# Gate and number operations of a mixture-of-experts kernel in groups of four tiles, and the adds of output pairs one operation a step

## The chip, the core and the metric

The kernel runs on one NeuronCore of a Trainium2 chip, as one program. The metric is the device time in microseconds. Before the change three runs took 502.27, 503.56 and 506.07 us; their median is 503.56 us.

The engines run their own instruction streams and wait for one another through semaphores: TensorE (PE: matrix products), VectorE (DVE), ScalarE (ACT), GpSimd (POOL) and SyncE (SP), which here only issues DMAs.

## The reference, cut to what matters

```
x = x + gnn(layernorm(x), adj)          # 4096 nodes, 256 features, adjacency 4096 x 4096
# ffn(layernorm(x)): 8 experts, the best two for each node
logits = xf @ Wg + bg
topk_scores, topk_idx = top_k(logits, 2)
topk_w = softmax(topk_scores)
h = gelu(einsum('nd,edh->neh', xf, W1) + b1)
y = einsum('neh,ehf->nef', h, W2) + b2
sel = take_along_axis(y, topk_idx[:, :, None], axis=1)
out = sum(topk_w[:, :, None] * sel, axis=1)
x = x + out
```

The kernel computes an expert only for the rows that chose it.

## The kernel before, in words

The first 350 us make the graph layer, choose the experts and write each node's row twice to a DRAM buffer, `dispatched`, sorted by expert: the row (as two f16 parts), its destination number (TOK), its first choice (EXP0), the weight of the first choice (W0) and the difference of the two weights (DW).

The expert stage then runs over ET = 39 tiles of 256 sorted rows, in steps numbered t, software-pipelined by hand; the order on each engine is that of the code, one step after the other:

- SP, `load_rows(t)`: loads tile t's rows to slot t % 8 of `erow` (shown as `stage` in the trace; erow, ehid, ehl and exT all lie in it). From t = 8 on it waits until tile t - 8 is transposed (s_etp) and its gates and numbers are made (s_idc).
- TensorE, step t: transposes tile t (L1329), hidden product of tile t - 1 (L1342, 12 matmuls), output product of tile t - 2 (L1362, 12 matmuls).
- VectorE, step t: COPY of the transposed tile t (L1114); output rows of tile t - 3 with scale and bias into `ysb` (L1122, shown as `rows`); low f16 part of the hidden values of tile t - 1 (L1129, waits for ScalarE's L776); then the gate operations of tile j = t - 1: L1137 and L1142 make `gate`, the weight of each row, and L1139 makes `enum`, the row of `pair_out` that the result goes to. `combine(k)`, in steps 32, 33, 35, 36 and 38 for groups 0 to 4 and behind step 41 for groups 5 and 6, adds the two expert results of 512 nodes (group k) to `x_sb`, with one operation for each (L1153, L1155).
- ScalarE, step t: GELU of tile t (L771, two operations), high f16 part (L776), then `gate_rows(t - 2)`: the output rows times their gates (L760, two operations; waits for L1122 and s_idc).
- GpSimd, `scatter(t)`: two indirect DMAs (L651) that write the 256 weighted rows of tile t to `pair_out` in DRAM. It waits for ScalarE's L760 and s_idc.

Behind the tiles, `pair_out` is read back in NG = 8 groups of 512 nodes (`load_pairs(k)` on SP, L510; the last in two halves, L513) to a ring of four buffers (in `z_lo` and `maskT`), when all tiles that can hold rows of it are scattered and, from k = 4 on, when group k - 4 is added (s_o2). SP's order is: loads 0 to 3 between the last row loads; load 4, write 0; load 5, writes 1, 2; load 6, writes 3, 4, 5; load 7; write 6; write of the last group's halves. `write_out(k)` (L519) waits for the second add of group k. The final group is added in halves (L1169, L1171).

Of the kernel before, what the change touches and what calls it, by code (L numbers as in the profile page):

```python
# [6 lines left out]
ALU = mybir.AluOpType  # L7
# [9 lines left out]
P = 128  # L17
# [6 lines left out]
def gnn_moe_kernel(nc, x, adj, W_self, b_self, W_nb, b_nb, W_comb, b_comb, Wg, bg, W1, b1, W2, b2, out):  # L24
# [47 lines left out]
    with ExitStack() as ctx:  # L72
# [112 lines left out]
        RY = 8  # L185
        tab = sb("tab", [P, 2, ET], I32)
        padrow = sb("padrow", [P, E], I32)
        enum = sb("enum", [P, RY, 2], I32)
        gate2 = sb("gate2", [P, 2, 2], F32)
        gate = sb("gate", [P, RY, 2], F32)  # L190
# [253 lines left out]
        def _(sp):  # L444
# [34 lines left out]
            def load_rows(t):  # L479
                if t == 0:  # L480
                    sp.wait_ge(s_sc[0], 16 * NT)
                if t == EA:
                    sp.wait_ge(s_dum, 16 * DUM)
                    sp.wait_ge(s_padw, 16 * E)
                    sp.wait_ge(s_tab, 4)
                    sp.wait_ge(s_sc[1], 16 * NT)
                if t == R:
                    sp.wait_ge(s_padr, 1)
                    for e in range(E):
                        write_pad(sp, e)  # L490
                a = t % R
                if t >= R:
                    sp.wait_ge(s_etp, t - R + 1)
                    sp.wait_ge(s_idc, t - R + 1)
                    apart(sp)
                row = sp.value_load(tab[0:1, 0, at(t)], min_val=0, max_val=ROWS - TT)
                sp.dma_start(erow_f[:, a], xs_dram[bass.ds(row, TT), :].rearrange("(p s) n -> p s n", s=2)).then_inc(s_er[a], 16)
                if t == R - 1:
                    sp.wait_ge(s_mm, NT)
                    sp.dma_start(b2_bc[:, :, :].rearrange("p e n -> p (e n)"),  # L500
                                 b2.rearrange("(o e) n -> o (e n)", o=1).to_broadcast((P, E * H))).then_inc(s_b2, 16)
# [33 lines left out]
        def _(pool):  # L535
# [110 lines left out]
            def scatter(t):  # L646
                a = t % RY
                pool.wait_ge(s_idc, t + 1)
                pool.wait_ge(s_gt, t + 1)
                for s in range(2):  # L650
                    gp.indirect_dma_start(  # L651
                        out=yp_dram[:, :], out_offset=bass.IndirectOffsetOnAxis(ap=enum[:, a, s:s + 1], axis=0),
# [7 lines left out]
        def _(act):  # L660
# [93 lines left out]
            def gate_rows(j):  # L754
                a = j % RY
                act.wait_ge(s_ey, j + 1)
                act.wait_ge(s_idc, j + 1)
                apart(act)
                for s in range(2):
                    last = sc.activation(ysb[:, a, s, :], ysb[:, a, s, :], ACT.Copy, scale=gate[:, a, s:s + 1])  # L760
# [32 lines left out]
        def _(dve):  # L793
# [313 lines left out]
            def expert_step(t, u, known):  # L1107
# [17 lines left out]
                if live(known, 1, ET):  # L1125
# [7 lines left out]
                    a, b = j % RY, j % R  # L1133
                    if j >= RY:
                        dve.wait_ge(s_ysc[a], 32 * (j // RY))
                    apart(dve)
                    v.scalar_tensor_tensor(gate2[:, r, :], erow32[:, b, :, EXP0], texp[:, at(j)], erow_f[:, b, :, DW],  # L1137
                                           ALU.not_equal, ALU.mult).then_inc(s_g2, 1)
                    v.scalar_tensor_tensor(enum[:, a, :], erow32[:, b, :, EXP0], texp[:, at(j)], erow32[:, b, :, TOK],  # L1139
                                           ALU.not_equal, ALU.add)  # L1140
                    dve.wait_ge(s_g2, j + 1)
                    v.tensor_tensor(gate[:, a, :], gate2[:, r, :], erow_f[:, b, :, W0], ALU.add).then_inc(s_idc, 1)  # L1142
                if known == 1:
                    table_late()
                if known in COMBINE:
                    combine(COMBINE.index(known))

            COMBINE = (32, 33, 35, 36, 38, 41)

            def combine(k):  # L1150
                dve.wait_ge(s_yl[k % Y], 16 * (k // Y + 1))
                xk = x_sb[:, B * k:B * k + B, :]
                v.tensor_tensor(xk, xk, yin[k % Y][:, :, 0, :], ALU.add).then_inc(s_o1, 1)  # L1153
                dve.wait_ge(s_o1, k + 1)
                v.tensor_tensor(xk, xk, yin[k % Y][:, :, 1, :], ALU.add).then_inc(s_o2, 1)  # L1155
# [7 lines left out]
            for k in range(len(COMBINE), NG - 1):  # L1163
                combine(k)
# [231 lines left out]
```

## Time and profile before

| | |
|---|---|
| median of three runs | 503.56 us |
| profiled execution, in all | 508.38 us |
| its span, first to last instruction | 505.0 us |
| TensorE busy | 436.5 us, 86% |
| VectorE busy | 371.1 us, 73% |
| GpSimd busy | 334.5 us, 66% |
| ScalarE busy | 259.7 us, 51% |
| mean granted TensorE clock | 0.946 |

A timeline row gives the start in us from the span's start, the duration, the engine, the line of the kernel, the operation, output and input names, and, in brackets, how long the engine had been idle before it and what ended this. A line L1129 is line 1129 of the kernel before. The engines overlap consecutive instructions, so the start of one to the start of the next tells what it occupies, not its duration. The 39 steps of the expert stage lie between 350 and 485 us of the span.

### The profile page before, as it was taken

What the parts mean: (1) busy time and instruction counts of PE and PEld (TensorE: products, weight loads), DVE (VectorE), ACT (ScalarE), POOL (GpSimd) and SP (SyncE); (2) the same over time, 40 slices, a digit from 0 to 9 for tenths busy, and PEclk for the clock granted to TensorE, in tenths of its full rate; (3) what the DMA queues carried; (4) which work ended last, traced back from release to release, by engine and by line L of the source; (5) the groups of instructions that cost most, each with busy time, mean ns of one, the idle gap of its engine ahead of it and who ended that gap; (6) DMA issues with size and microseconds to landing.
All of it is one profiled execution on the core that took longest, in us unless ns stands there. A gap on an engine that the chain in (4) does not pass through costs nothing.

```text
span 505.0 us, 12812 instructions
## 1 busy us (share of the span) xinstructions
PE 436.5 (86%) x4214; PEld 384.7 (76%) x4214; DVE 371.1 (73%) x1056; ACT 259.7 (51%) x403; POOL 334.5 (66%) x348
## 2 busy tenths in 40 slices
PE   5789999889999889999979969964899999997710
PEld 5678988778888778988858858863799999996610
DVE  2898754577878977798569489766777777779972
ACT  2666872245543524344434443233588888886620
POOL 3498586165666877778658756366788788885570
PEclk9999999999999979999989979985799999999985
DMA  8997899889996999899999997196865556598665
GB/s 222 278 302 230 214 234 286 223 247 264 275 278 181 311 265 257 245 276 291 298 279 275 291 301 216 43 297 209 286 199 174 174 173 186 174 324 346 195 218 166
DMA packets 48687, 122.47 MB, mean 243 GB/s; under 512 B 10601, under 2 KB 19693, under 8 KB 47600
## 3 DMA queue, kind: packets, MB, share of 16 engines
q1 hardware_dynamic: 26736, 64.09, 44.6%
q0 software_dynamic: 16144, 50.49, 33.8%
q10 hardware_dynamic: 5744, 7.08, 5.1%
q8 instruction: 35, 0.57, 0.5%
q14 instruction: 28, 0.23, 0.2%
HBM read 96.52 MB, written 26.93 MB: 244 GB/s over the span
## 4 chain that ended last, share of the span: by engine, by line
DVE 34%; PE 16%; ACT 15%; DMA 13%; issue 10%; POOL 8%; ACTq 2%; DVEq 1%; POOLq 1%; SPq 0%
DMA wst<-in_L_ffn_W_dram 11%; PE bank L1245 7%; ACT stage L771 7%; DVE maskT L845 5%; DVE stage L1129 5%; ACT stage L776 4%; POOL rs L633 3%; DVE x_sb L930 2%; DVE xh L928 2%; DVE w L982 2%; DVE st L934 2%; PE bank L1236 2%; ACT xh L725 2%; PE bank L1237 2%; PE bank L1362 2%
## 5 line engine op out<-in xcount | busy, mean ns | idle before, releaser
L1236 PE MATMUL bank<-z_flat,maskT 128*128 128x257 f16 x1024 | 232.9, 278 | 8.5 <-issue 8.5
L1237 PE MATMUL bank<-z_lo,maskT 128*128 128x256 f16 x1024 | 232.7, 277 | 0.0
L1236 PEld LDWEIGHTS bank<-z_flat,maskT 128*128 128x128 fp8e4 x1024 | 101.9, 100 | 22.9 <-issue 9.0
L651 POOL DMA_INDIRECT pair_out<-rows,enum x78 | 93.6, 1199 | 33.3 <-issue 21.3
L1237 PEld LDWEIGHTS bank<-z_lo,maskT 128*128 128x128 fp8e4 x1024 | 101.8, 99 | 13.2
L676 ACT ACTIVATE mask<-stage,m 128x2048 fp8e4<-128x2048 int32 x32 | 64.1, 2002 | 58.7 <-DMA stage<-in_adj_dram,gidx 47.5
L584 POOL DMA_INDIRECT dispatched<-rows,slot x64 | 65.0, 1016 | 29.4 <-issue 18.2
L573 POOL DMA_INDIRECT stage<-in_adj_dram,gidx x64 | 65.7, 1027 | 26.1 <-issue 13.6
L633 POOL TENSOR_TENSOR rs<-ve,mhalf 128x1 f32<-128x1 f32 x32 | 39.0, 1220 | 49.9 <-DVE ve L939 49.8
L725 ACT ACTIVATE xh<-x_sb,nb,rs 128x256 f32<-128x256 f32 x32 | 19.2, 599 | 100.7 <-POOL nb L635 80.0
L1342 PE MATMUL bank<-stage,w 128*128 128x256 f16 x468 | 59.8, 279 | 4.8 <-DVE stage L1114 4.8
L1362 PE MATMUL bank<-w,stage 128*128 x468 | 57.6, 273 | 3.0 <-DVE stage L1129 2.8
L771 ACT ACTIVATE stage<-bank,b1c,sc 128x256 f32<-128x256 f32 x78 | 43.2, 562 | 21.0 <-PE bank L1342 9.7
L1342 PEld LDWEIGHTS bank<-stage,w 128*128 x468 | 45.2, 100 | 11.1 <-issue 5.5
L1362 PEld LDWEIGHTS bank<-w,stage 128*128 128x128 f16 x468 | 45.3, 98 | 9.4 <-issue 3.8
L1129 DVE SCALAR_TENSOR_TENSOR stage<-stage,shs 128x512 f16<-128x512 f32 x39 | 29.3, 750 | 26.1 <-ACT stage L776 25.7
L1245 PE MATMUL bank<-wf,w 128*128 128x256 f16 x384 | 43.9, 273 | 3.7 <-DVE wf L882 1.8
L838 DVE TENSOR_SCALAR mask<-stage 128x2048 fp8e4<-128x2048 int32 x32 | 39.9, 1246 | 6.3 <-DMA stage<-in_adj_dram 6.3
L1245 PEld LDWEIGHTS bank<-wf,w 128*128 128x128 f16 x384 | 37.3, 98 | 8.7 <-DVE wf L882 2.2
L845 DVE STREAM_TRANSPOSE maskT<-mask 128x1024 uint32<-128x1024 uint32 x32 | 39.6, 1236 | 3.1 <-PE bank L1237 3.1
L760 ACT ACTIVATE rows<-rows,gate 128x256 f32<-128x256 f32 x78 | 34.9, 494 | 10.0 <-DVE rows L1122 10.0
L915 DVE TENSOR_TENSOR rows<-xh,rows 128x256 f16<-128x256 f32 x32 | 14.4, 451 | 27.6 <-ACT rows L728 27.6
(179 smaller groups left out, 607.8 us busy)
## 6 DMA issues: line engine op xcount, KB each, us to landing
stage<-in_adj_dram SPq DMA_DIRECT2D x256, 128.0 KB, 6.4
stage<-dispatched SPq DMA_DIRECT2D x39, 260.0 KB, 3.2
wst<-in_L_ffn_W_dram ACTq DMA_DIRECT2D x16, 256.0 KB
z_lo<-pair_out SPq DMA_DIRECT2D x4, 1024.0 KB, 7.8
dispatched<-pad SPq DMA_DIRECT2D x15, 260.0 KB, 5.2
out_dram<-x_sb SPq DMA_DIRECT2D x28, 128.0 KB
maskT<-pair_out SPq DMA_DIRECT2D x3, 1024.0 KB, 9.4
x_sb<-in_x_dram ACTq DMA_DIRECT2D x6, 256.0 KB, 11.3
```

Source lines behind the costliest of these rows:

```text
L573: gp.indirect_dma_start(out=stage[:, s, b - 2, :], out_offset=None, in_=adj_q[:, :], in_offset=bass.IndirectOffsetOnAxis(ap=gidx[:, 0:1], ...
L584: gp.indirect_dma_start(out=xs_dram[:, :], out_offset=bass.IndirectOffsetOnAxis(ap=slot[:, t, c:c + 1], axis=0), in_=rows_f[:, t, :], in_o ...
L651: gp.indirect_dma_start(out=yp_dram[:, :], out_offset=bass.IndirectOffsetOnAxis(ap=enum[:, a, s:s + 1], axis=0), in_=ysb[:, a, s, :], in_o ...
L676: sc.activation(mask[:, u % 2, 2:4, :], stage[:, s], ACT.Sigmoid, bias=m100[:, 0:1], scale=200.0, saturate=False).then_inc(s_mA, 1)
L771: sc.activation(ehid[:, u % 2, h, :], hps[2 * (u % 2) + h][:, 0:TT], ACT.Gelu, bias=b1c[:, bass.ds(ex, 1), h], scale=sc1[:, bass.ds(ex, 1) ...
L845: v.transpose(maskT32[u % 4], mask32[u % 2]).then_inc(s_T, 1)
L1129: v.scalar_tensor_tensor(ehl[:, r, 1].rearrange("p t n -> p (t n)"), ehid[:, r].rearrange("p t n -> p (t n)"), shs[:, bass.ds(ex, 1)], ehl ...
L1236: mm(acc[u % 2][:, 0:D + 1], a, z_hi[:, i, :], start=(i == 0), stop=False)
L1237: last = mm(acc[u % 2][:, 0:D], a, z_lo[:, i, :], start=False, stop=(i == NT - 1))
L1245: last = mm(out_, lhs(xp * KT + kt), w(wp, kt), start=(first and n == 0), stop=(final and n == 3 * KT - 1))
L1342: last = mm(hps[2 * r + h][:, 0:TT], w, exT[:, r, (xp * KT + kt) * TT:(xp * KT + kt + 1) * TT], start=(n == 0), stop=(n == 3 * KT - 1))
L1362: last = mm(fold[r][:, s * H:s * H + H], ehl[:, r, xp, kt, s * P:s * P + P], w, start=(n == 0), stop=(n == 3 * KT - 1))
```

## The change

Two parts, both in VectorE's program of the expert stage.

First, the gate operations are made for four tiles at once, in step j + 1 for j = 0, 4, 8, ... (`gates(j, n)`): the comparison of EXP0 with the tile's expert goes to a tile of its own (`other`), from which `enum` and `gate2` are made, and `gate` from `gate2`. That is four operations of 8 elements a partition for four tiles, where there were three of 2 elements for each. The group waits for the rows of all its tiles. `enum` and `gate` have 16 slots and not 8. SP, ScalarE and GpSimd wait for the group that a tile belongs to.

Second, `combine(k)` is cut in two: `add_first(k)` and `add_second(k)`. Groups 0 to 3 are added in steps 32 to 39, one operation a step; groups 4 to 6 behind step 41, that is behind the last output rows.

```
-        RY = 8
+        RY, RE, GT = 8, 16, 4
...
-                    sp.wait_ge(s_idc, t - R + 1)
+                    sp.wait_ge(s_idc, (t - R) // GT + 1)
...
-                pool.wait_ge(s_idc, t + 1)
+                pool.wait_ge(s_idc, t // GT + 1)
...
-                act.wait_ge(s_idc, j + 1)
+                act.wait_ge(s_idc, j // GT + 1)
...
-                    a, b = j % RY, j % R
-                    if j >= RY:
-                        dve.wait_ge(s_ysc[a], 32 * (j // RY))
-                    apart(dve)
-                    v.scalar_tensor_tensor(gate2[:, r, :], erow32[:, b, :, EXP0], texp[:, at(j)], erow_f[:, b, :, DW],
-                                           ALU.not_equal, ALU.mult).then_inc(s_g2, 1)
-                    v.scalar_tensor_tensor(enum[:, a, :], erow32[:, b, :, EXP0], texp[:, at(j)], erow32[:, b, :, TOK],
-                                           ALU.not_equal, ALU.add)
-                    dve.wait_ge(s_g2, j + 1)
-                    v.tensor_tensor(gate[:, a, :], gate2[:, r, :], erow_f[:, b, :, W0], ALU.add).then_inc(s_idc, 1)
+                    if j % GT == 0:
+                        gates(j, min(GT, ET - j))
                 if known == 1:
                     table_late()
-                if known in COMBINE:
-                    combine(COMBINE.index(known))
-
-            COMBINE = (32, 33, 35, 36, 38, 41)
-
-            def combine(k):
+                if 0 <= t - ADD_FROM < 2 * ADDED:
+                    (add_first, add_second)[(t - ADD_FROM) % 2]((t - ADD_FROM) // 2)
+
+            def gates(j, n):
+                m, b, e = j // GT, j % R, j % RE
+                for i in range(j, j + n):
+                    dve.wait_ge(s_er[i % R], 16 * (i // R + 1))
+                    if i >= RE:
+                        dve.wait_ge(s_ysc[i % RY], 32 * ((i - RE) // RY + 1))
+                apart(dve)
+                v.tensor_tensor(other[:, m % 2, 0:n, :], erow32[:, b:b + n, :, EXP0],
+                                texp[:, j:j + n].rearrange("p (t o) -> p t o", o=1).to_broadcast((P, n, 2)),
+                                ALU.not_equal).then_inc(s_g2, 1)
+                dve.wait_ge(s_g2, 2 * m + 1)
+                v.tensor_tensor(enum[:, e:e + n, :], other[:, m % 2, 0:n, :], erow32[:, b:b + n, :, TOK], ALU.add)
+                v.tensor_tensor(gate2[:, m % 2, 0:n, :], other[:, m % 2, 0:n, :], erow_f[:, b:b + n, :, DW], ALU.mult).then_inc(s_g2, 1)
+                dve.wait_ge(s_g2, 2 * m + 2)
+                v.tensor_tensor(gate[:, e:e + n, :], gate2[:, m % 2, 0:n, :], erow_f[:, b:b + n, :, W0], ALU.add).then_inc(s_idc, 1)
+
+            ADDED, ADD_FROM = NG // 2, 32
+
+            def add_first(k):
                 dve.wait_ge(s_yl[k % Y], 16 * (k // Y + 1))
                 xk = x_sb[:, B * k:B * k + B, :]
                 v.tensor_tensor(xk, xk, yin[k % Y][:, :, 0, :], ALU.add).then_inc(s_o1, 1)
+
+            def add_second(k):
                 dve.wait_ge(s_o1, k + 1)
+                xk = x_sb[:, B * k:B * k + B, :]
                 v.tensor_tensor(xk, xk, yin[k % Y][:, :, 1, :], ALU.add).then_inc(s_o2, 1)
...
-            for k in range(len(COMBINE), NG - 1):
-                combine(k)
+            for k in range(ADDED, NG - 1):
+                add_first(k)
+                add_second(k)
```

VectorE's order in step 33, from its L1129 (tile 32) to that of step 34, before:

```order
L1129 SCALAR_TENSOR_TENSOR stage<-stage,shs 128x512
L1137 SCALAR_TENSOR_TENSOR gate<-stage,texp 128x2
L1139 SCALAR_TENSOR_TENSOR enum<-stage,texp 128x2
L1142 TENSOR_TENSOR gate<-gate,stage 128x2
L1153 TENSOR_TENSOR x_sb<-x_sb,z_lo 128x1024
L1155 TENSOR_TENSOR x_sb<-x_sb,z_lo 128x1024
L1114 COPY stage<-bank 128x1024
```

The same place of the changed kernel, and the step behind it (L1130 is the old L1129, L1115 the COPY, L1123 the output rows, L1162 the first add, L1167 the second):

```order
L1130 SCALAR_TENSOR_TENSOR stage<-stage,shs 128x512
L1148 TENSOR_TENSOR other<-stage,texp 128x8
L1152 TENSOR_TENSOR enum<-other,stage 128x8
L1153 TENSOR_TENSOR gate<-other,stage 128x8
L1155 TENSOR_TENSOR gate<-gate,stage 128x8
L1167 TENSOR_TENSOR x_sb<-x_sb,z_lo 128x1024
L1115 COPY stage<-bank 128x1024
L1123 ISA
L1123 SCALAR_TENSOR_TENSOR rows<-bank,sc,z_flat 128x2x256
L1128 TENSOR_LOAD tab
L1128 ISA x2
L1130 ISA
```

Step 33 holds one add, not two, and the gates of tiles 32 to 35; steps 34 to 36 then hold no gate operation.

VectorE's order behind the gate operations of tile 38, up to the last group, before:

```order
L1122 ISA
L1122 SCALAR_TENSOR_TENSOR rows<-bank,sc,z_flat 128x2x256
L1122 ISA
L1122 SCALAR_TENSOR_TENSOR rows<-bank,sc,z_flat 128x2x256
L1153 TENSOR_TENSOR x_sb<-x_sb,z_lo 128x1024
L1155 TENSOR_TENSOR x_sb<-x_sb,z_lo 128x1024
L1153 TENSOR_TENSOR x_sb<-x_sb,maskT 128x1024
L1155 TENSOR_TENSOR x_sb<-x_sb,maskT 128x1024
L1169 TENSOR_TENSOR x_sb<-x_sb,maskT 128x512
```

And of the changed kernel:

```order
L1167 TENSOR_TENSOR x_sb<-x_sb,maskT 128x1024
L1123 ISA
L1123 SCALAR_TENSOR_TENSOR rows<-bank,sc,z_flat 128x2x256
L1123 ISA
L1123 SCALAR_TENSOR_TENSOR rows<-bank,sc,z_flat 128x2x256
L1162 TENSOR_TENSOR x_sb<-x_sb,z_lo 128x1024
L1167 TENSOR_TENSOR x_sb<-x_sb,z_lo 128x1024
L1162 TENSOR_TENSOR x_sb<-x_sb,z_lo 128x1024
L1167 TENSOR_TENSOR x_sb<-x_sb,z_lo 128x1024
L1162 TENSOR_TENSOR x_sb<-x_sb,maskT 128x1024
L1167 TENSOR_TENSOR x_sb<-x_sb,maskT 128x1024
L1182 TENSOR_TENSOR x_sb<-x_sb,maskT 128x512
```

Six adds stand between the last output rows (L1123 of tile 38) and the last group, where four stood; the last add of group 3 has moved ahead of the output rows of tile 37. The order on the other engines and queues is unchanged; only the numbers that they wait for on s_idc differ.

## Rows read from the trace of the kernel before

**Rows 1.** Busy us by engine: stretch, length, busy (instructions), then clock, DMA, GB/s.

```profile
400.00:430.00 30.00, 30.00 (x317) 27.35 (x315) 22.81 (x60) 25.92 (x50) 24.21 (x20) 1.00 0.59 178
460.00:478.00 18.00, 13.79 (x135) 11.26 (x134) 16.19 (x31) 11.01 (x22) 9.27 (x9) 1.00 0.70 249
```

**Rows 2.** Timeline, one steady step on TensorE and VectorE.

```profile
422.19 1.47 PE L1342 MATMUL bank<-stage,w 128*128 128x256 f16 x12
422.30 0.75 DVE L1129 SCALAR_TENSOR_TENSOR stage<-stage,shs 128x512 f16<-128x512 f32 x1 [0.72 <-ACT stage L776]
422.97 0.22 DVE L1137 SCALAR_TENSOR_TENSOR gate<-stage,texp 128x2 f32<-128x2 int32 x1
...
423.24 0.15 DVE L1142 TENSOR_TENSOR gate<-gate,stage 128x2 f32<-128x2 f32 x1
423.31 0.68 DVE L1114 COPY stage<-bank 128x1024 f16<-128x1024 f16 x1
...
423.50 1.47 PE L1362 MATMUL bank<-w,stage 128*128 x12
423.91 0.74 DVE L1122 SCALAR_TENSOR_TENSOR rows<-bank,sc,z_flat 128x512 f32<-128x512 f32 x1
...
425.26 1.47 PE L1342 MATMUL bank<-stage,w 128*128 128x256 f16 x12
```

**Rows 3.** Timeline, VectorE, the end of step 32 and the COPYs after it.

```profile
452.97 0.75 DVE L1129 SCALAR_TENSOR_TENSOR stage<-stage,shs 128x512 f16<-128x512 f32 x1 [0.72 <-ACT stage L776]
...
453.97 1.22 DVE L1153 TENSOR_TENSOR x_sb<-x_sb,z_lo 128x1024 f32<-128x1024 f32 x1
...
456.37 0.68 DVE L1114 COPY stage<-bank 128x1024 f16<-128x1024 f16 x1
...
461.02 0.68 DVE L1114 COPY stage<-bank 128x1024 f16<-128x1024 f16 x1
```

**Rows 4.** Timeline: TensorE behind the COPY of step 33, VectorE in step 35.

```profile
457.20 1.53 PE L1342 MATMUL bank<-stage,w 128*128 128x256 f16 x12 [1.11 <-DVE stage L1114]
...
465.80 0.75 DVE L1129 SCALAR_TENSOR_TENSOR stage<-stage,shs 128x512 f16<-128x512 f32 x1 [1.19 <-ACT stage L776]
```

**Rows 5.** Timeline, VectorE, from tile 38's output rows to the last group.

```profile
484.72 0.75 DVE L1122 SCALAR_TENSOR_TENSOR rows<-bank,sc,z_flat 128x512 f32<-128x512 f32 x1 [0.68 <-PE bank L1362]
485.39 1.27 DVE L1153 TENSOR_TENSOR x_sb<-x_sb,z_lo 128x1024 f32<-128x1024 f32 x1
...
486.69 1.25 DVE L1155 TENSOR_TENSOR x_sb<-x_sb,z_lo 128x1024 f32<-128x1024 f32 x1
...
498.47 0.69 DVE L1169 TENSOR_TENSOR x_sb<-x_sb,maskT 128x512 f32<-128x512 f32 x1 [8.13 <-DMA maskT<-pair_out]
```

**Rows 6.** Timeline, ScalarE's weighting of tile 36 and four of the last scatters.

```profile
482.38 0.91 ACT L760 ACTIVATE rows<-rows,gate 128x256 f32<-128x256 f32 x2 [1.86 <-DVE rows L1122]
...
484.12 0.98 POOL L651 DMA_INDIRECT pair_out<-rows,enum  x1 [1.64 <-ACT rows L760]
...
486.69 0.98 POOL L651 DMA_INDIRECT pair_out<-rows,enum  x1 [0.30 <-ACT rows L760]
...
487.98 1.96 POOL L651 DMA_INDIRECT pair_out<-rows,enum  x1 [0.31 <-issue]
...
491.54 0.98 POOL L651 DMA_INDIRECT pair_out<-rows,enum  x1 [0.30 <-issue]
```

**Rows 7.** Chain of waits: start us, us, what; the last pair load.

```profile
493.85 4.60 DMA maskT<-pair_out
```

**Rows 8.** Timeline, VectorE, two small operations in a chain.

```profile
339.76 0.16 DVE L925 RECIPROCAL rdeg<-sdeg 128x1 f32<-128x1 f32 x1
340.02 0.48 DVE L928 SCALAR_TENSOR_TENSOR xh<-bank,rdeg,rows 128x256 f32<-128x256 f32 x1
```

**Rows 9.** Timeline, SP, the loads of tiles 10 and 11.

```profile
371.43 1.51 SPq L497 DMA_DIRECT2D stage<-dispatched  x2
```

**Rows 10.** Timeline, SP, the four DMAs of one group's write.

```profile
456.93 1.86 SPq L519 DMA_DIRECT2D out_dram<-x_sb  x4
```

More of the change, by code:

```diff
@@ L184, in gnn_moe_kernel @@
         tileP = sb("tileP", [P, 1], F32)
-        RY = 8
+        RY, RE, GT = 8, 16, 4
         tab = sb("tab", [P, 2, ET], I32)
         padrow = sb("padrow", [P, E], I32)
-        enum = sb("enum", [P, RY, 2], I32)
-        gate2 = sb("gate2", [P, 2, 2], F32)
-        gate = sb("gate", [P, RY, 2], F32)
+        enum = sb("enum", [P, RE, 2], I32)
+        other = sb("other", [P, 2, GT, 2], F32)
+        gate2 = sb("gate2", [P, 2, GT, 2], F32)
+        gate = sb("gate", [P, RE, 2], F32)
         pad = sb("pad", [P, 1, RW], F32)
@@ L651, in scatter @@
                     gp.indirect_dma_start(
-                        out=yp_dram[:, :], out_offset=bass.IndirectOffsetOnAxis(ap=enum[:, a, s:s + 1], axis=0),
+                        out=yp_dram[:, :], out_offset=bass.IndirectOffsetOnAxis(ap=enum[:, t % RE, s:s + 1], axis=0),
                         in_=ysb[:, a, s, :], in_offset=None, bounds_check=2 * N - 1, oob_is_err=False).then_inc(s_ysc[a], 16)
@@ L756, in gate_rows @@
                 act.wait_ge(s_ey, j + 1)
-                act.wait_ge(s_idc, j + 1)
+                act.wait_ge(s_idc, j // GT + 1)
                 apart(act)
                 for s in range(2):
-                    last = sc.activation(ysb[:, a, s, :], ysb[:, a, s, :], ACT.Copy, scale=gate[:, a, s:s + 1])
+                    last = sc.activation(ysb[:, a, s, :], ysb[:, a, s, :], ACT.Copy, scale=gate[:, j % RE, s:s + 1])
                 last.then_inc(s_gt, 1)
```

## The prediction

> **What bounds the kernel now.** I read the busy time by stretch first. From 400 to 430 us TensorE is busy 30.00 of 30 us at a granted clock of 1.00, VectorE 22.81; from 460 to 478 us TensorE is down to 13.79 of 18 and VectorE is at 16.19 [rows 1]. So the expert stage has two parts with different bounds.
>
> In the steady part a step is 3.07 us: one hidden-layer product at 422.19, the next at 425.26. Its two products take 1.31 us of issue each and the transposes the other 0.44, so TensorE has no gap. VectorE waits 0.72 us in each step, ahead of L1129 [rows 2]. (The chain of waits goes through ScalarE and L1129 here, but by the code L771 of a tile waits for the product of its own tile and for the L1129 of two tiles earlier, long done. TensorE sets the pace.) From 453 us on VectorE also adds the expert outputs of a pair group, two operations of 1.22 us in one step. A step with them goes from one COPY at 456.37 to the next at 461.02, 4.65 us, with no idle, and TensorE waits 1.11 us for the COPY [rows 3, 4].
>
> Then the end. The last output row operation (L1122, tile 38) starts at 484.72; its six scatter operations on GpSimd (tiles 36 to 38) start from 484.12 to 491.54; the last group of pairs is loaded at 493.85 and lands 4.60 us later; VectorE, idle for 8.13 us, adds it at 498.47 [rows 5 to 7]. The four adds of groups 5 and 6 (the first at 485.39, the second at 486.69) lie beside these scatters.
>
> **Gates, four tiles at once.** Before, the three small operations hold VectorE from 422.97 to 423.31, 0.34 us a step [rows 2], 1.36 for four tiles. Now there are four, two of which wait for the one before. Two such small operations in a chain start 0.26 us apart at 339.76 and 340.02 [rows 8]; two unchained ones start 0.13 apart and the last is followed 0.07 later. So 0.26 + 0.13 + 0.26 + 0.07, about 0.7; the operands are 8 wide and not 2, which I take as nothing, with 1.0 as the upper bound for the added semaphore waits. I use 0.65 to 0.7. Saved: 0.65 us of VectorE in four steps. In the steady part it buys nothing: it lengthens a 0.72 us idle. With that cover gone, from step 32 on, it counts in full. The one step in four that is 0.35 longer still ends its COPY some 0.9 us ahead of the product that reads it (423.99 against 425.26, less 0.35).
>
> The group waits for the rows of up to three tiles ahead. The rows of tiles 10 and 11 are issued from 371.43 to 372.94 [rows 9]; the group of tiles 8 to 11 comes in step 9, behind the L1129 that lies 23 steps of 3.07 ahead of the one at 452.97 [rows 3], at 382.4. Some 6 us of slack even if a load takes the page's 3.2 us, and later loads now wait for the transposes only, so they start earlier. Cost nothing.
>
> **One add a step.** Between L1129 at 452.97 and the COPY at 456.37 lie 0.67 of L1129, 0.33 of gates and two adds: an add is 1.2 us of VectorE. COPY is 0.60 to the next start (423.31 to 423.91), L1122 and L1129 0.66 each (2.25 with the gates' 0.33 for a step of 4.65 less two adds). A step with one add is 0.60 + 0.66 + 0.66 + 1.2 = 3.12, against TensorE's 3.07: the gap in TensorE goes nearly. Group 0 now starts with one add in step 32, so the COPY of step 33 comes at 452.97 + 0.67 + 1.2 = 454.84 (was 456.37). Steps 33 to 38 then take 6 x 3.12, and 2 x 0.65 for the gate groups in steps 33 and 37: 20.0, to 474.9. I add 0.5 for waits, because ScalarE's round is long: from COPY at 461.02 to L1129 of the same tile at 465.80 is 4.78 us [rows 3, 4], and two steps must hold it, L1129 and an add (6.65, or 7.3 with gates, against 6.24 and 6.9). So step 39 begins at 475.4. Its L1129 (tile 38) waits for ScalarE: COPY of step 38 at 472.2, plus 4.65, a little under the 4.78 above since ScalarE holds less there, is 476.85; L1129 0.67 and the last of the eight adds 1.2 give 478.7; then L1122 of tiles 37 and 38, 0.66 apart: **tile 38 at 479.4, was 484.72, 5.3 us earlier.** Bounds: 477, where TensorE alone paces (15 more products 3.07 apart from 425.26 put tile 38's at 471.3; its L1129 comes 3.2 later, as 422.30 + 3.07 does after 422.19; the output product and its landing take some 2.6, an estimate from twice 1.31), and 482 if each of the eight steps loses another 0.3 us.
>
> **Behind the last output.** GpSimd: ScalarE weights tile 36's rows behind its copy of tile 38, which ends at 476.7. This takes 0.9 us and the first scatter starts 0.83 us later, as 484.12 does after 482.38 + 0.91 [rows 6]: 478.4. From that scatter to the last load there were 9.73 us [rows 6, 7]; the same spacing gives 488.1. If all six operations take 0.98 plus 0.30 and wait only for their own tiles (L1122 of tile 37 at 478.7, so its scatters from 481.3), the last scatter starts 3 x 1.28 later, and the load 2.31 behind it (491.54 to 493.85): 487.5. I take 487.8.
> The SP queue: six adds now stand behind tile 38, not four. Ahead of the last load SP must issue the writes of groups 3, 4 and 5, the last of which waits for the fourth of these adds: 0.67 + 3 x 1.24 + 1.24 = 5.65 after L1122 starts [rows 5], so 485.05, and its four DMAs take 1.86 [rows 10]: 486.9, just ahead of the scatters. The six adds end at 487.5, ahead of the last load's landing; they are hidden. Thus the last load is issued at about **487.8 against 493.85: 6.1 us earlier**. It now starts 1 us behind 0.5 MB of writes, where before 4 us lay between (the add that they wait for ended at 486.69 + 1.25, and 1.86 for the issues); no row shows such a load, so it costs from 0 to 2 us; I take 0.3, since a landing takes 4.60 us for 0.5 MB and most of that is latency that the writes drain in. What follows the landing is unchanged.
>
> Sum: 6.1 - 0.3 = 5.8 us off the span, 505.0 to 499.2. The profiled execution took 508.38 in all, 3.38 around the span, and lies 1% over the median of 503.56; where those 4.8 us are no row tells, so the sum is a difference, good for either: 508.38 less 5.8 is 502.6, and off the median it is **497.8 us**.
>
> **The rivals.**
> (a) GpSimd holds the gain back. For: the scatter at 487.98 lasted 1.96 us under two adds and the steady second one lasts longer than its first. Against: the one at 486.69 starts together with an add and took 0.98 [rows 6]. If the four scatters of tiles 37 and 38 that lie under the six adds each took 1.96, the load would come 3 x 0.98 later than 487.8 (one such stretch is in the old spacing): 490.7, a gain of 2.8, time 500.8.
> The Trainium skill, SBUF — State Buffer, section "Two separate sides", says that a VectorE operation with two SBUF inputs and a GpSimd operation that reads SBUF exclude each other for the whole instruction. By it each of the four would wait for an add to end, which gives case (a) or worse; the trace agrees at 487.98 and disagrees at 486.69.
> (b) The steps don't speed up: VectorE is not what paces steps 32 to 39 but ScalarE's round. Then tile 38 stays at 482 to 484.7, and the last load at 490.4 to 493.85; time 500.4 to 503.6, next to no change. Against: the steps with adds show no VectorE idle.
> (c) Slower: with VectorE full in eight steps running, a wait (for a pair group's landing in the first add, which now stands in every second step) is no longer absorbed and is paid by every later step. It decides from 1.4 us a step on: 8 x 1.4 = 11.2 eats the 5.8 and 5.4 more, 509.0. Against: the first add at 453.97 shows no idle ahead of it [rows 3], groups 1 to 3 are now wanted two steps apart and so later than before, and groups 4 to 6 only behind tile 38.
>
> **How the numbers follow.** Forecast 0.65, with its own range 495.4 to 500.2 (tile 38 from 477 to 482 moves the end by 2.4 either way); (a) 0.17; (b) 0.13; (c) 0.05. Faster by over 1% means under 498.5 (1% is about what a measurement of this kernel can tell from no change, as its own runs spread from 502.27 to 506.07): four fifths of the forecast, 0.52. Within 1%: the rest of it, (a) and (b), and a part of (c), 0.43. Slower 0.05. The range takes (a) and half of (b) in, and at the low end the bound where TensorE paces: 494.8 to 501.9.
>
> **What would show it.** Right: steady steps still 3.07 us with VectorE's idle about 0.9 to 1.0 in three steps of four; gate groups holding VectorE 0.65 to 0.7; COPY to COPY 3.1 to 3.2 from step 33 on (3.8 with gates), with TensorE nearly without idle; tile 38's L1122 about 25 us after the COPY of step 33 (28.35 before); the last pair load some 8.4 us after that L1122 (9.13 before). Wrong: scatters over 1.5 us each in the last 10 us (a), idle ahead of L1129 in steps 33 to 38 (b), or idle ahead of the first adds (c).

## The result and the profile after

The changed kernel took 497.58 us (median of four runs, 494.73 to 499.87) against 502.91 us for the kernel before on the same chip (501.84 to 506.07): a ratio of 0.986, 95% interval 0.982 to 0.990. The forecast was 497.8 us. All ratios here leave out three slow executions (508.56 and 2516.53 us of the kernel before, 777.69 us of the kernel with all adds behind).

| | before | after |
|---|---|---|
| profiled execution, in all | 508.38 us | 497.83 us |
| its span | 505.0 us | 495.7 us |
| TensorE busy | 436.5 us | 432.9 us |
| VectorE busy | 371.1 us | 362.2 us |
| GpSimd busy | 334.5 us | 321.8 us |

The two spans differ by 9.3 us, but not all of that is the change. The first COPY of the expert stage starts at 349.19 in the trace before and at 345.33 in the trace after, and up to that place the two programs are the same. In the traces of all kernels run here it lies between 344.6 and 349.2. So a place is needed from which to count. I take the start of the hidden product of tile 31 on TensorE, the last one that no add of any kernel here can have delayed, since TensorE has no gap up to it: from the third product on they start 3.06 to 3.07 us apart in every trace. Before:

```profile
449.79 1.47 PE L1342 MATMUL bank<-stage,w 128*128 128x256 f16 x12
```

And after:

```profile
446.48 1.47 PE L1355 MATMUL bank<-stage,w 128*128 128x256 f16 x12
```

From there to the end of the span it is 55.21 us before and 49.22 after, 5.99 us less.

Busy time by stretch, after (columns as in [rows 1]):

```profile
400.00:430.00 30.00, 30.00 (x316) 27.34 (x315) 20.85 (x41) 25.94 (x50) 19.01 (x21) 1.00 0.53 164
430.00:460.00 30.00, 29.92 (x314) 26.92 (x313) 23.61 (x41) 25.12 (x48) 19.45 (x20) 1.00 0.88 298
460.00:478.00 18.00, 12.38 (x117) 10.00 (x114) 17.34 (x25) 12.64 (x26) 13.94 (x12) 1.00 0.76 247
```

In the steady part TensorE is full as before, and VectorE has 2 us less to do in 30, which buys nothing. From 460 to 478 VectorE is now full (17.34 of 18).

VectorE's timeline after, from the end of step 32 to the COPY of step 35:

```profile
449.65 0.75 DVE L1130 SCALAR_TENSOR_TENSOR stage<-stage,shs 128x512 f16<-128x512 f32 x1 [1.06 <-ACT stage L777]
450.33 1.21 DVE L1162 TENSOR_TENSOR x_sb<-x_sb,z_lo 128x1024 f32<-128x1024 f32 x1
451.46 0.68 DVE L1115 COPY stage<-bank 128x1024 f16<-128x1024 f16 x1
...
453.39 0.16 DVE L1148 TENSOR_TENSOR other<-stage,texp 128x8 f32<-128x8 int32 x1
453.58 0.17 DVE L1152 TENSOR_TENSOR enum<-other,stage 128x8 int32<-128x8 f32 x1
453.67 0.17 DVE L1153 TENSOR_TENSOR gate<-other,stage 128x8 f32<-128x8 f32 x1
453.87 0.17 DVE L1155 TENSOR_TENSOR gate<-gate,stage 128x8 f32<-128x8 f32 x1
453.96 1.22 DVE L1167 TENSOR_TENSOR x_sb<-x_sb,z_lo 128x1024 f32<-128x1024 f32 x1
455.09 0.68 DVE L1115 COPY stage<-bank 128x1024 f16<-128x1024 f16 x1
...
458.15 0.68 DVE L1115 COPY stage<-bank 128x1024 f16<-128x1024 f16 x1
```

A gate group holds VectorE from 453.39 to 453.96, 0.57 us. A step with one add and no group is 458.15 - 455.09 = 3.06 us, where the step with two adds had been 4.65 [rows 3].

The end of the chain of waits after (start us, us, what):

```profile
476.90 0.24 POOL pair_out L652
...
481.74 2.86 DMA pair_out<-rows,enum
...
485.20 5.46 DMA maskT<-pair_out
490.67 0.02 issue
490.69 0.70 DVE x_sb L1182
```

The last scatter starts at 481.74 and lands 2.86 us later; the load of the last pairs is issued at 484.81; its first half is added at 489.10, its second at 490.69. The idle ahead of the first is 6.10 us, where it had been 8.13 [rows 5]. SP's timeline, this load:

```profile
484.81 0.82 SPq L514 DMA_DIRECT2D maskT<-pair_out  x2
```

### The profile page after: what moved, and what is told of

The parts are those of the page before. It is cut to its first block, busy times and chain, and to the rows that moved or that the text cites. A ratio compares the mean times of both kernels' runs of the same rounds, so it can differ in the third digit from the quotient of the medians.

```text
span 495.7 us, 12735 instructions
## 1 busy us (share of the span) xinstructions
PE 432.9 (87%) x4214; PEld 382.7 (77%) x4214; DVE 362.2 (73%) x979; ACT 260.3 (53%) x403; POOL 321.8 (65%) x348
## 4 chain that ended last, share of the span: by engine, by line
DVE 31%; PE 27%; DMA 16%; issue 8%; POOL 8%; ACT 4%; SPq 1%; DVEq 1%; ACTq 1%; POOLq 0%
PE bank L1355 9%; PE bank L1375 8%; DMA wst<-in_L_ffn_W_dram 8%; PE bank L1258 7%; DVE maskT L846 5%; POOL rs L634 3%; PE bank L1342 3%; DVE x_sb L931 3%; DMA x_sb<-in_x_dram 2%; DMA stage<-in_adj_dram,gidx 2%; DVE xh L929 2%; DVE w L983 2%; DVE st L935 2%; DMA stage<-in_adj_dram 2%; ACT xh L726 2%
## 5 line engine op out<-in xcount | busy, mean ns | idle before, releaser
L1249 PE MATMUL bank<-z_flat,maskT 128*128 128x257 f16 x1024 | 229.5, 276 | 8.4 <-issue 8.3
L1250 PE MATMUL bank<-z_lo,maskT 128*128 128x256 f16 x1024 | 229.3, 275 | 0.0
L652 POOL DMA_INDIRECT pair_out<-rows,enum x78 | 81.0, 1038 | 40.2 <-ACT rows L761 17.8
L634 POOL TENSOR_TENSOR rs<-ve,mhalf 128x1 f32<-128x1 f32 x32 | 40.1, 1254 | 48.8 <-DVE ve L940 48.6
L1130 DVE SCALAR_TENSOR_TENSOR stage<-stage,shs 128x512 f16<-128x512 f32 x39 | 29.3, 751 | 31.3 <-ACT stage L777 30.9
L916 DVE TENSOR_TENSOR rows<-xh,rows 128x256 f16<-128x256 f32 x32 | 15.4, 480 | 28.3 <-ACT rows L729 28.3
## 6 DMA issues: line engine op xcount, KB each, us to landing
maskT<-pair_out SPq DMA_DIRECT2D x3, 1024.0 KB, 11.4
x_sb<-in_x_dram ACTq DMA_DIRECT2D x6, 256.0 KB, 10.5
```

What stands on the lines that cost most here:

```text
L634: gp.tensor_tensor(rs[:, t:t + 1], ve[:, t:t + 1], mhalf[:, 0:1], ALU.pow).then_inc(s_rs2, 1)
L652: gp.indirect_dma_start(out=yp_dram[:, :], out_offset=bass.IndirectOffsetOnAxis(ap=enum[:, t % RE, s:s + 1], axis=0), in_=ysb[:, a, s, :], ...
L1249: mm(acc[u % 2][:, 0:D + 1], a, z_hi[:, i, :], start=(i == 0), stop=False)
L1250: last = mm(acc[u % 2][:, 0:D], a, z_lo[:, i, :], start=False, stop=(i == NT - 1))
```

## The experiments

All landmarks, in us after the hidden product of tile 31, one profiled execution each. "Tile 38" is the start of its output rows, "GpSimd" the first scatter of tile 36 and the last of tile 38, "load" the issue of the last pair load, "end" the end of the span. Where the trace shows the last two output rows as one entry (the changed kernel: 474.21, 1.50 us for both), the second is taken to last 0.74 us and its start is reckoned back from their end. Ratios are to the kernel before, on the same chip.

| kernel | COPY 33 | COPY 38 | tile 38 | GpSimd | load | end | ratio (95%) |
|---|---|---|---|---|---|---|---|
| before | 6.58 | 26.31 | 34.93 | 34.33 to 41.75 | 44.06 | 55.21 | 1 |
| changed | 4.98 | 21.57 | 28.49 | 27.84 to 35.26 | 38.33 | 49.22 | 0.986 (0.982 to 0.990) |
| gates alone | 6.24 | 25.64 | 34.80 | 33.11 to 40.42 | 42.73 | 53.71 | 0.997 (0.994 to 1.000) |
| adds alone | 5.31 | 22.26 | 29.53 | 28.64 to 36.31 | 39.04 | 50.00 | 0.988 (0.984 to 0.993) |
| writes behind | 4.98 | 21.69 | 28.73 | 27.65 to 35.44 | 37.75 | 52.13 | 0.996 (0.993 to 0.999) |
| adds wait | 4.98 | 21.81 | 28.84 | 29.33 to 35.77 | 38.08 | 52.21 | 0.994 (0.991 to 0.998) |
| all adds behind | 3.85 | 19.74 | 26.75 | 26.10 to 33.53 | 48.03 | 60.66 | 1.011 (1.007 to 1.015) |
| groups of two | 4.97 | 22.12 | 29.59 | 28.51 to 36.37 | 39.12 | 50.02 | 0.987 (0.982 to 0.991) |
| eight from 31 | 4.98 | 21.63 | 28.69 | 27.63 to 34.31 | 38.48 | 49.66 | 0.987 (0.983 to 0.991) |
| three from 31 | 4.97 | 20.28 | 27.70 | 27.09 to 34.51 | 37.29 | 48.21 | 0.986 (0.982 to 0.990) |
| changed, again | 4.98 | 21.41 | 28.45 | 28.94 to 36.36 | 38.67 | 49.89 | 0.990 (0.985 to 0.995) |
| three from 31, again | 4.98 | 20.85 | 28.80 | 28.15 to 35.57 | 38.38 | 49.55 | 0.986 (0.982 to 0.991) |

The expectations below count from the COPY of step 32 instead. It turned out to be a bad landmark, because the change itself moves it: it comes 1.12 us after that product in the kernel before and with the adds alone (1.11), 0.77 in the kernels whose step 31 holds no gate operations, 1.32 with groups of two, and 1.91 where step 31 holds an add. For a comparison with a number in an expectation these are to be taken off.

### The two parts apart

Gates alone: the changed kernel with both adds of a group in one step, at the old places.

```
-                if 0 <= t - ADD_FROM < 2 * ADDED:
-                    (add_first, add_second)[(t - ADD_FROM) % 2]((t - ADD_FROM) // 2)
+                if known in COMBINE:      # (32, 33, 35, 36, 38, 41)
+                    k = COMBINE.index(known)
+                    add_first(k)
+                    add_second(k)
```

> The gate groups alone, with the old places of the adds (steps 32, 33, 35, 36, 38, behind 41). From the sum: the groups save 0.65 us of VectorE in four steps, so about 1.3 us over steps 32 to 39, and nothing in the steady part; the load of the last pairs comes about 1 us earlier, time 0.998 of before. In the steady part the step stays 3.07 us. Rival, that the gates are most of the gain (by making the gates of a tile early and by freeing GpSimd, whose second scatter of a tile lasts 1.47 us before and 0.98 in the changed kernel): the last scatter comes 3 us or more earlier, ratio 0.994 or less.

Adds alone: the kernel before with its three gate operations a tile, and the new schedule of the adds.

```
-                if known in COMBINE:
-                    combine(COMBINE.index(known))
+                if 0 <= t - ADD_FROM < 2 * ADDED:
+                    (add_first, add_second)[(t - ADD_FROM) % 2]((t - ADD_FROM) // 2)
```

> The adds alone, one operation a step for groups 0 to 3 and 4 to 6 behind the last output, with the old three gate operations a tile. From the sum: the last output rows come 4.5 to 5 us earlier than before, counted from the COPY of step 32, and the time is 0.990 to 0.991 of before, most of the change. Rival, that the scatters stay slow (1.47 us for the second of a tile, 3.05 a tile) and hold the end back: the last output comes early but the last load gains less than 3 us, ratio 0.994 or more.

Measured: 0.997 and 0.988, whose product, 0.985, is that of both within the intervals. The gates alone brought the last load from 44.06 to 42.73, 1.3 us, and the adds alone to 39.04, 5.0 us. With the adds alone the last output rows came 5.4 us earlier (29.53), a little more than expected; with the gates alone 0.1 us (34.80). So the adds are nearly all of the change; neither rival holds.

That the gates alone moved the last output rows by 0.1 us and the load by 1.3 has a reason in the trace: VectorE's L1130 of tile 38 came 1.2 us earlier than before, and so did tile 36's scatters, but TensorE's last product took 2.59 us where it took 1.50 in every other trace:

```profile
481.13 2.59 PE L1377 MATMUL bank<-w,stage 128*128 x12 [2.24 <-DVE stage L1130]
```

The granted clock was 0.84 from 480 to 482 us and 0.50, the lower level of 1.2 GHz, from 482 to 484, behind an idle of 2.24 us. (Before, the idle was 2.55 us there and the clock stayed at 1.00.)

The rival to the first rested on the second scatter of a tile, 1.47 us in the steady part before and 0.98 after. In this kernel with the old gate operations it is 0.98 as well, GpSimd's timeline:

```profile
419.70 0.98 POOL L651 DMA_INDIRECT pair_out<-rows,enum  x1 [0.79 <-DVE gate L1142]
420.98 0.99 POOL L651 DMA_INDIRECT pair_out<-rows,enum  x1 [0.30 <-issue]
422.76 0.98 POOL L651 DMA_INDIRECT pair_out<-rows,enum  x1 [0.79 <-DVE gate L1142]
```

So the old gate operations are not enough to lengthen it; the last section comes back to it.

### Does SP's queue or GpSimd hold the last load?

Writes behind: groups 3, 4 and 5 are written behind the last load.

```
-                for done in {4: (0,), 5: (1, 2), 6: (3, 4, 5)}.get(k, ()):
+                for done in {4: (0,), 5: (1, 2), 7: (3, 4, 5)}.get(k, ()):
```

> The changed kernel with SP's writes of groups 3, 4 and 5 moved behind the load of the last pairs. If the queue at SP had held that load, it would now be issued earlier. In the changed kernel's trace the writes are issued by 482.3 and the load at 484.81 behind the last scatter at 481.74 + 2.86, so GpSimd's scatters hold it and I expect the same time within 0.3%, with the landing perhaps 0.5 to 1 us shorter (5.5 to 4.6 us) for want of writes in the queues, and the end set by the 12 writes issued later: up to 2 us worse. Rival (the writes in flight slow the scatters' landing and the load): 1 us or more faster.

Measured: the load is issued at 37.75, 0.6 us earlier, although the last scatter starts no earlier (35.44): from its start to the load it took 2.31 us here and 3.07 in the changed kernel, where SP had issued its writes 2.5 us ahead of the load and was waiting. So the queue at SP did not hold the load. The writes in flight seem to lengthen the scatter's landing: this time is 2.31 us in the five traces in which the last write ahead of the load had been issued before the last scatter started (before, gates alone, writes behind, adds wait, and the changed kernel's repeat), and 2.73 to 3.07 in the five in which SP was still issuing it. (With eight from 31 the last scatter was itself a long one, and with all adds behind the load waits for adds.) But the end came 2.9 us later, and the ratio went to 0.996: the writes now stand between the load and the end. SP's timeline, the 16 DMAs of the four writes and then the last half's:

```profile
485.72 0.82 SPq L514 DMA_DIRECT2D maskT<-pair_out  x2
486.59 9.69 SPq L520 DMA_DIRECT2D out_dram<-x_sb  x16
496.32 2.05 SPq L434 DMA_DIRECT2D out_dram<-x_sb  x4
```

This is worse than I expected (2 us at most, and the same time within 0.3%): the issue of these 16 DMAs took SP 9.69 us, and the last half's write stood behind it. The landing of the last load's first half was 4.56 us (485.72 to 490.28), no shorter than the changed kernel's 4.29.

Adds wait: as this kernel, and the adds of groups 4 to 6 wait for the last scatter's landing.

```
+            for a in range(RY):
+                dve.wait_ge(s_ysc[a], 32 * -(-(ET - a) // RY))
             for k in range(ADDED, NG - 1):
```

> As the run with the writes behind the last load, and the six adds of groups 4 to 6 wait until all scatters have landed. Nothing but the scatters then runs on VectorE's or GpSimd's side in the last 7 us. If the adds lengthen scatters (one of 1.96 us in both traces), the last six scatters take 0.98 each and the last load comes 1 us or more earlier after the last output rows. If they don't, one scatter near the end is still 1.5 to 2 us. The whole is slower than the run with the writes behind by 1 to 3 us, as the adds now run into the landing of the last load (six of 1.24 us are 7.5, the landing 4.6 to 5.5).

Measured: GpSimd's last six scatters, with no add beside them:

```profile
475.22 0.98 POOL L652 DMA_INDIRECT pair_out<-rows,enum  x1 [0.30 <-issue]
476.51 0.98 POOL L652 DMA_INDIRECT pair_out<-rows,enum  x1 [0.30 <-issue]
477.80 0.98 POOL L652 DMA_INDIRECT pair_out<-rows,enum  x1 [0.30 <-issue]
479.08 0.98 POOL L652 DMA_INDIRECT pair_out<-rows,enum  x1 [0.30 <-issue]
480.37 0.98 POOL L652 DMA_INDIRECT pair_out<-rows,enum  x1 [0.31 <-issue]
481.66 0.98 POOL L652 DMA_INDIRECT pair_out<-rows,enum  x1 [0.30 <-issue]
```

And in the changed kernel, with the adds beside them:

```profile
476.90 0.98 POOL L652 DMA_INDIRECT pair_out<-rows,enum  x1 [0.30 <-ACT rows L761]
476.90 1.25 DVE L1167 TENSOR_TENSOR x_sb<-x_sb,z_lo 128x1024 f32<-128x1024 f32 x1
478.07 1.21 DVE L1162 TENSOR_TENSOR x_sb<-x_sb,z_lo 128x1024 f32<-128x1024 f32 x1
478.18 1.96 POOL L652 DMA_INDIRECT pair_out<-rows,enum  x1 [0.30 <-issue]
...
480.45 0.98 POOL L652 DMA_INDIRECT pair_out<-rows,enum  x1 [0.31 <-issue]
480.46 1.25 DVE L1162 TENSOR_TENSOR x_sb<-x_sb,maskT 128x1024 f32<-128x1024 f32 x1
```

From first to last the six take 6.44 us without adds and 7.42 with them; in every kernel with adds beside the last scatters one of these takes 1.86 to 2.00 us, one and not four (in two of them another takes 1.22 or 1.36). Rival (a) is thus real in kind and a quarter of its size. The long one is the one that starts behind an add, by 0.11 us here and by 0.08 to 0.21 elsewhere; those that start together with an add, or just ahead of it, take 0.98. The last section takes this up. The load itself came only 0.25 us earlier than in the changed kernel, since four earlier scatters, beside the single adds in the steps, were longer here (1.87, 2.02, 1.46 and 1.63 us, where the changed kernel had 1.46, 0.99, 0.98 and 1.48) and the six began later (29.33); so it was 0.3 us later than with the writes behind, where the theory had said 1 us earlier. The whole was 1.5 us shorter by median and 0.1 longer in the trace than the kernel with the writes behind, not 1 to 3 us longer: those writes hid the adds' delay.

### What paces the steps?

All adds behind: `ADDED = 0`, fourteen adds behind the last output rows.

```
-            ADDED, ADD_FROM = NG // 2, 32
+            ADDED, ADD_FROM = 0, 32
```

> The changed kernel with all fourteen adds of groups 0 to 6 behind the last output rows, none in the steps. The steps then show what TensorE and ScalarE alone allow: by the lower bound of the prediction the last output rows start 26.1 us after the COPY of step 32, with steps of 3.07 us to the end. GpSimd's scatters then last 0.98 us each up to the last output. The end is later than the changed kernel's by 8 us or more, as loads 4 to 7 now wait for adds. Rival (ScalarE's round paces the steps, case b): the last output rows stay at 27.5 us or later.

Measured: 26.75 after the product of tile 31, that is 25.98 after the COPY of step 32 (expected 26.1), with the last output product waiting for VectorE's L1130, and this for ScalarE. VectorE's timeline from step 39 on:

```profile
469.93 0.75 DVE L1130 SCALAR_TENSOR_TENSOR stage<-stage,shs 128x512 f16<-128x512 f32 x1 [1.20 <-ACT stage L777]
470.60 0.74 DVE L1123 SCALAR_TENSOR_TENSOR rows<-bank,sc,z_flat 128x512 f32<-128x512 f32 x1
472.49 0.75 DVE L1123 SCALAR_TENSOR_TENSOR rows<-bank,sc,z_flat 128x512 f32<-128x512 f32 x1 [1.14 <-PE bank L1375]
```

So 26.75 is where TensorE and ScalarE alone put the last output rows, and the changed kernel, at 28.49, is 1.7 us behind it; rival (b) falls. One scatter ahead of all adds, at 470.10, took 1.44 us and not 0.98: an add is not needed for a long one. But the kernel as a whole takes 1% more than before, because the loads of groups 4 to 7 wait for adds.

Groups of two: `GT = 2`.

> The changed kernel with gate groups of two tiles and not four: the same four operations twice as often. The cost of a group does not depend on its width (0.65 to 0.7 us), so the gates cost 0.33 us a tile as before the change; the steps 33 to 38 together get 0.65 us longer than with groups of four, and the last output rows come at about 28.4 us after the COPY of step 32 (27.72). Rival (width counts): a group of two holds VectorE clearly less than 0.57 us.

Measured: a group of two holds VectorE 0.55 us, as one of four does (0.57), so width does not count. The COPY of step 38 came 0.55 us later than with groups of four (22.12, 21.57) and tile 38 1.1 us later (29.59, the same as with the old gates, 29.53). The ratio, from two executions, can't be told from the changed kernel's.

### A better place for the adds

Eight from 31: `ADD_FROM = 31`, else the changed kernel.

> The changed kernel with its eight single adds in steps 31 to 38 in place of 32 to 39. VectorE's last output rows wait in step 40 for TensorE and ScalarE, not for the add of step 39, so tile 38 gains 0.3 us at most, tile 37 up to 1 us; the last load stays within 0.5 us, as GpSimd works through its backlog. Ratio within 0.3% of the changed kernel's 0.988. Rival (the add of step 39 held the end): the last load 1 us or more earlier.

Three from 31: six single adds, in steps 31 to 36, four groups behind the last output rows, and the write of group 5 behind the last load.

```
-            ADDED, ADD_FROM = NG // 2, 32
+            ADDED, ADD_FROM = 3, 31
...
-                for done in {4: (0,), 5: (1, 2), 6: (3, 4, 5)}.get(k, ()):
+                for done in {4: (0,), 5: (1, 2), 6: (3, 4), 7: (5,)}.get(k, ()):
```

> The changed kernel with only groups 0 to 2 added one operation a step, from step 31 on (so steps 31 to 36), groups 3 to 6 behind the last output, and the write of group 5 moved behind the load of the last pairs. VectorE's sum: one add more falls into the idle of step 31, steps 37 and 38 hold none, so the last output rows come 1 to 1.5 us earlier after the COPY of step 32 than the changed kernel's 27.72 us, and fewer scatters lie under adds ahead of it. The last load then comes 1 to 1.5 us earlier than 37.56 and the ratio to before is 0.985 to 0.987. Rival, that GpSimd alone sets the end: the last scatter stays within 0.4 us and the ratio at 0.988.

Measured: counted as I had counted, from the COPY of step 32, the ends came 0.7 and 2.15 us sooner than the changed kernel's. But an add in step 31 delays that COPY by 1.1 us. Counted from the product of tile 31, eight from 31 gains nothing (tile 38 at 28.69, the load at 38.48, the end at 49.66 against 28.49, 38.33 and 49.22), as expected; three from 31 has tile 38 at 27.70, 0.8 us earlier, the load at 37.29 and the end at 48.21, 1.0 us sooner. The ratios on their chip are 0.987 and 0.986. To tell this from the changed kernel's, both ran once more on one chip:

> The changed kernel itself, beside the next run on the same chip. By its first trace and the prediction: ratio to before 0.986 to 0.989. The span up to the COPY of step 32 differs from run to run by up to 4 us (447.25 in its first trace, 446.1 to 451.3 in the other kernels), the rest of the span, 48.45 us, should repeat within 0.5 us. Rival (the adds' place also moves the stage's start): the rest differs as much as the first part.

> The kernel with groups 0 to 2 added in steps 31 to 36 and the write of group 5 behind the last load, beside the changed kernel on one chip. Its first trace ended 46.30 us after the COPY of step 32 against 48.45: I expect 2 us less than the changed kernel, a ratio to before lower by 0.004. Rival (the 2 us are one execution's): the same ratio.

Measured: the changed kernel 499.66 us, ratio 0.990, end at 49.89 (49.22 the first time, 0.67 apart and so a little outside the 0.5 expected); three from 31: 498.32 us, ratio 0.986, end at 49.55 (48.21). The medians lie as expected but the intervals (0.985 to 0.995 and 0.982 to 0.991) overlap, and in the second pair of traces the gain from the product of tile 31 on is 0.34 us, no more than the same kernel differs from itself. The 2 us that I had expected were the landmark's. Three from 31 beats the kernel before in both measurements; that it beats the changed kernel is not shown.

## Why the prediction was right

**Steady part: right.** The product-to-product step stays 3.07 us and TensorE is busy 30.00 of 30; VectorE's idle ahead of L1130 is 1.06 us in steps without a group (0.9 to 1.0 was said) and 0.48 behind one.

**The gates: right.** A group takes 0.57 us, not 0.65 to 0.7: the starts in it are 0.19, 0.09, 0.20 and 0.09 apart, where I had taken 0.26 for the chained ones from an operation that reads a reciprocal [rows 8]. At the old places of the adds the groups are worth 1.3 us at the last load, as by the sum. Beside adds dealt out one a step they are worth less: the load moved by 0.7 us (39.04 to 38.33), and by 0.4 if the repeat of the changed kernel is taken (38.67), no more than one kernel differs from itself; the ratios of adds alone and of both parts can't be told apart either.

**One add a step: right, and the steps are 1.1 us better than forecast.** The COPY of step 33 came at 4.98 (forecast 454.84 - 449.79 = 5.05). The step is then 3.06 us and not 3.12, as a single add holds VectorE for 1.13 to 1.14 us and not 1.2: of two adds in a row the second waits for the first and starts 1.26 behind it, which a single one does not. The 0.5 us for ScalarE's round was hardly needed (0.11 us in step 37). Tile 38: forecast 479.4 - 449.79 = 29.6, measured 28.49, 6.4 us earlier than before where 5.3 was forecast.

**Behind the last output: right in kind, the saving there over-sized.** The load came at 38.33, forecast 487.8 - 449.79 = 38.0: 5.7 us earlier, not 6.1, although GpSimd had its tiles 0.8 us earlier (27.84, forecast 28.6). From tile 36's first scatter to the load it took 10.49 us, not the 9.73 of before: the scatters took the same 7.42, but from the start of the last one to the load it was 3.07 and not 2.31. GpSimd, and not the queue at SP, held the load: the writes ahead of it were issued by 482.3, the load at 484.81.

So one of the signs named in the prediction failed: the load comes 9.84 us after tile 38's L1123, where some 8.4 was said and 9.13 had been before. The forecast let tile 36's scatters wait for ScalarE. In the changed kernel GpSimd has no idle longer than 0.31 us from 471.25 on, and two of its scatters there take 1.48 and 1.96 us; it paces the end itself, and what tile 38 gains beyond this is lost.

**The last load's landing.** I took 0.3 us for the writes just ahead of it. Its first half was added 4.29 us after the issue (4.62 before), so it cost nothing; but its second half landed at 490.67, and VectorE waited 0.17 us for it, which it had not before. From the issue of the load to the end of the span it took 10.89 us, 11.15 before: 0.3 us gained where 0.3 had been forecast as lost.

Sum: the rest of the span shrank by 5.99 us; forecast 5.8. The steps gained 1.1 us more than forecast and the last load's landing 0.6 us more; the way from tile 38 to the load took 1.4 us more than forecast. That these cancel, and the sum came out within 0.2 us, is luck; the mechanism, VectorE's lumps of two adds as what paces the last steps, is not. The profiled executions' 508.38 to 497.83 would have suggested 10.5, and the medians 5.3. Of the 10.5 us, 3.3 lie ahead of the product of tile 31 and 1.3 outside the span, where the change does nothing. To take the sum off the median was right for this reason.

**The rivals.** (a) is real at one scatter in six, 1 us, in the kernel before too, and so no loss. The scatter at 486.69, which the prediction held against the skill's page, starts at the same time as its add, and not behind it (last section). (b) fell: the last output rows left 34.93 for 28.49. (c) did not occur: the first adds show no idle ahead of them, and TensorE's longest waits from step 33 on are 0.85 us for the COPY of step 38 and 1.56 us ahead of its last product, where before it waited four times 1.02 to 1.39 us for a COPY and 2.55 us ahead of the last product.

## What to carry to other kernels

When one engine has slack in a steady loop and is full at its end, look at how extra work is dealt out: a lump of two additions stalls the pipelined engine behind it, while single ones mostly fill the slack. Here eight single adds put the last output rows 1.7 us behind where they come with none (28.49 and 26.75), and ten in lumps of two, with the old gates, 8.2 us (34.93).

Not all of that is the dealing. Ten adds stood ahead of the last output rows before and eight after, and no run deals the same eight in twos. The two that went behind are 2.4 us of VectorE at most [rows 3], so of the 5.4 us that the adds alone brought at least 3.0 belong to the dealing; this is an estimate.

To start one step earlier (31) brought nothing that the runs show. Put what has a later deadline behind the last output, beside the DMAs that are waited for anyway, but no more than fits there: with all fourteen adds behind it the end came 11.4 us later. And count a change's effect from a landmark that it can't move: up to the first COPY of the stage the programs are the same, and its place differed by up to 4.5 us, while my first landmark, which the edits did move, invented a gain of 1.1 us.

## What the runs showed of the hardware

GpSimd's scatters have two modes in the steady part, which I had not expected. In four of the twelve traces (before, adds wait, three from 31, groups of two) the second scatter of a tile takes 1.47 us, the mean is 1229 to 1235 ns and GpSimd never waits for an engine; in the other eight every scatter takes 0.98 us and GpSimd waits for ScalarE or the gates in each tile. The same kernel shows both. From 380 to 436 us, three from 31, the first time:

```profile
L652 POOL DMA_INDIRECT pair_out<-rows,enum x37 | 45.7, 1235 | 11.3 <-issue 11.3
```

And again:

```profile
L652 POOL DMA_INDIRECT pair_out<-rows,enum x37 | 36.4, 983 | 20.1 <-ACT rows L761 10.3 <-issue 5.8 <-DVE gate L1155 4.0
```

The four are those in which GpSimd came to the first scatter late, straight from its work before (0.30 us of idle ahead of it, 0.47 to 1.49 in the other eight). The mode moved no other engine: the step is 3.07 us in both.

What decides is where a scatter starts. One that starts while VectorE is in an operation with two inputs from SBUF (L1129 or L1130, or an add) lasts until that operation lets go, 0.64 us after the start of L1129 or L1130 and 1.10 us after that of an add, and then its own 0.98 us. In the kernel before, 0.14 us behind the L1129 of 422.30 [rows 2]:

```profile
422.44 1.47 POOL L651 DMA_INDIRECT pair_out<-rows,enum  x1 [0.30 <-issue]
```

It ends at 423.91, and 422.30 + 0.64 + 0.98 is 423.92. The scatter at 478.18 of the changed kernel, 0.11 us behind the add of 478.07, ends at 480.14, and 478.07 + 1.10 + 0.98 is 480.15. With these two figures, which were fitted to the traces, the rule gives the duration of 930 of the 936 scatters in the twelve traces within 0.05 us. Of the other six, four are 2.55 us long (one at 459.59 in the changed kernel): they meet L1130 and then the add behind it. The last two start 0.04 and 0.06 us behind an operation, where it is not clear who is first. A scatter that starts together with such an operation or ahead of it takes 0.98 us, and so do over 300 that start within a COPY or within L1122 or L1123, which take an input from `bank`, TensorE's output.

This also explains why the mode of 1.47 us lasts. The second scatter starts some 0.14 us behind L1129 or L1130 and ends 1.62 us behind its start; 0.30 idle, the next tile's first scatter of 0.98 and 0.30 idle bring the next one to 3.20 us, which is 0.13 behind the L1129 or L1130 of the next step, 3.07 us on. In the other mode the scatters start 1.50 and 2.79 us behind L1130 and meet none. No run shifted this phase on purpose; the run in which the adds wait, whose last six scatters all take 0.98 us, is the only trial of the rule.

The Trainium skill, SBUF — State Buffer, section "Two separate sides", says that of the two, a VectorE operation with two SBUF inputs and a GpSimd operation that reads SBUF, whichever starts first has the shared ports for its whole instruction and the other waits. The traces agree where VectorE starts first. Where the scatter does, they don't: 76 adds that started while a scatter ran took 1.21 to 1.23 us, and the others 1.21 to 1.29.
